# Six transformer layers behind a cross attention: the layer loop written out, a new order of work in each slot, one half of the LayerNorm read in place

## What is computed

```python
x = x + tanh(g_xattn[0]) * xattn(layernorm(x), ctx, ctx, frac, ...)      # logits + alpha_pos*max(D,0) + alpha_neg*min(D,0), D = clip(frac_k - frac_q)
y = layernorm(x)
for i in range(6):
    y = attn_layer(shift_tokens(y), Wqkv[i], q_scale[i], k_scale[i], Wo[i]) + y
    y = ffn_layer(shift_tokens(y), ln_g[i], ln_b[i], W1[i], b1[i], W2[i], b2[i]) + y
x = x + tanh(g_ffn[0]) * y
# shift_tokens: the first 64 features of a token stay, the last 64 come from the token before
# attn_layer: 16 heads of 64; q and k are divided by their norms, scaled and rotated; each window of
#             32 tokens looks at itself and at the window before it; softmax; Wo
# ffn_layer: LayerNorm, W1 (2 x 341 columns), a * gelu(gate), W2
```

## Time and profile before

| | |
|---|---|
| median of three runs | 2069.49 us (2068.37 to 2073.53) |
| profiled execution, its own time | 2061.48 us |
| span from its first to its last instruction | 2059.7 us |
| PE busy / weight loads | 1797.2 us (87%) / 1401.8 us (68%) |
| VectorE / ScalarE / GpSimd busy | 1600.0 (78%) / 1384.6 (67%) / 1332.1 (65%) us |
| cross attention, about | 0 to 250 us |
| a layer, about | 297 to 299 us, six times |

### The profile page before, as it was taken

How to read it: one execution, slowest core, us unless ns; L and a number is a source line. 1 busy time by engine, 2 the same in 40 slices (tenths; PEclk the granted TensorE clock), 3 DMA queues, 4 the chain that set the end, 5 groups by cost and what they waited for, 6 DMA issues and landing times.

```text
span 2059.7 us, 86637 instructions
## 1 busy us (share of the span) xinstructions
PE 1797.2 (87%) x33584; PEld 1401.8 (68%) x33584; DVE 1600.0 (78%) x3772; ACT 1384.6 (67%) x3701; POOL 1332.1 (65%) x1226
## 2 busy tenths in 40 slices
PE   6999878998879898789988899988898988899887
PEld 3445457777667776677776677776677776677766
DVE  5766679898468987488896589885689885689984
ACT  3677657777557776567775577775577775577765
POOL 3444467777467777377775477774677773677773
PEclk9999979999989999999999999999899999899999
DMA  5000021111021111111110211110211110211111
GB/s 121 4 5 5 1 70 33 35 37 32 25 64 41 31 36 28 63 34 33 40 31 23 68 40 31 41 31 23 64 44 31 31 42 22 65 37 37 31 33 46
DMA packets 59120, 77.81 MB, mean 38 GB/s; under 512 B 16608, under 2 KB 31674, under 8 KB 57914
## 3 DMA queue, kind: packets, MB, share of 16 engines
q1 hardware_dynamic: 58938, 75.36, 13.9%
HBM read 22.63 MB, written 1.05 MB: 11 GB/s over the span
## 4 chain that ended last, share of the span: by engine, by line
PE 60%; DVE 15%; issue 12%; ACT 6%; POOL 5%; SPq 0%; DMA 0%; DVEq 0%; ACTq 0%; POOLq 0%
PE proj_ps L455 7%; PE s_ps L476 7%; PE tr_ps L465 7%; PE y_ps L524 7%; PE proj_ps L457 5%; PE proj_ps L456 5%; PE y_ps L516 4%; DVE by_cos L1091 3%; PE pv_ps L506 3%; ACT square L816 3%; DVE by_sin L1091 3%; DVE xs L1352 3%; PE s_ps L571 3%; DVE sumsq L1103 2%; PE s_ps L691 2%
## 5 line engine op out<-in xcount | busy, mean ns | idle before, releaser
L1502 POOL TENSOR_TENSOR qk<-by_cos,by_sin 128x512 f32<-128x512 f32 x388 | 495.3, 1276 | 208.3 <-DVE by_sin L1091 201.9
L1509 POOL TENSOR_TENSOR qk<-qk,inv_norm 128x512 f32<-128x512 f32 x388 | 404.8, 1045 | 68.7 <-ACT inv_norm L822 41.6
L1091 DVE TENSOR_TENSOR by_cos<-proj_ps,tab 128x512 f32<-128x512 f32 x364 | 249.4, 685 | 159.6 <-ACT square L816 158.6
L816 ACT ACTIVATE square<-proj_ps 128x512 f32<-128x512 f32 x364 | 217.4, 597 | 195.1 <-PE proj_ps L457 194.8
L1515 POOL TENSOR_TENSOR s_sb<-s_sb,row_max 128x512 f32<-128x512 f32 x192 | 202.7, 1056 | 136.1 <-DVE row_max L1122 136.1
L455 PE MATMUL proj_ps<-w_hi,x_hi 128*128 128x512 f32 x546 | 273.8, 502 | 4.8 <-DVE by_sin L1091 2.6
L465 PE MATMUL tr_ps<-ident,qk 128*128 128x128 f32 x1544 | 247.2, 284 | 24.2 <-ACT x_hi L810 11.8
L1103 DVE TENSOR_REDUCE sumsq<-square 128x8 f32<-128x512 f32 x388 | 262.2, 676 | 0.0
L1091 DVE TENSOR_TENSOR by_sin<-proj_ps,tab 128x512 f32<-128x512 f32 x364 | 247.8, 681 | 0.0
L465 PEld LDWEIGHTS tr_ps<-ident,qk 128*128 128x128 f32 x1544 | 184.0, 146 | 72.5 <-POOL qk L1509 28.5
L457 PE MATMUL proj_ps<-w_hi,x_lo 128*128 128x512 f32 x546 | 222.1, 407 | 0.0
(11 more groups left out here) (172 smaller groups left out, 4167.1 us busy)
## 6 DMA issues: line engine op xcount, KB each, us to landing
arena<-v SPq DMA_DIRECT2D x388, 130.0 KB, 2.4
w_raw<-in_L_ffn_Wqkv SPq DMA_DIRECT2D x7, 1536.0 KB, 7.3
wo<-in_L_ffn_Wo SPq DMA_DIRECT2D x7, 512.0 KB, 3.8
w_raw<-in_L_ffn_W SPq DMA_DIRECT2D x7, 341.0 KB, 5.5
c_in<-in_ctx SPq DMA_DIRECT2D x16, 64.0 KB, 1.8
xn<-in_fside_BxS SPq DMA_DIRECT2D x1, 1024.0 KB, 6.0
out<-z SPq DMA_DIRECT2D x4, 256.0 KB, 3.0
w<-in_L_ffn_W SPq DMA_DIRECT2D x12, 64.0 KB
```

Source lines behind the costliest of these rows:

```text
L1091: return dve.tensor_tensor(dst[:, c % 2, :].rearrange("p (h d) -> p h d", d=DH), ps, tb, ALU.mult)
L1502: pool.tensor_tensor(heads(qk[:, c, :]), heads(by_cos[:, c % 2, :]), heads(by_sin[:, c % 2, :])[:, :, ::-1, :], ALU.add).then_inc(qk_added, 1)
L1509: pool.tensor_tensor(ap, ap, inv_norm[:, c, :].unsqueeze(2).to_broadcast([128, 8, DH]), ALU.mult).then_inc(qk_ready, 1)
```

## The change

1. `for L in range(1, LAYERS + 1)` in place of `Fori` on all five engines: six copies of a layer's code in a row. The loops over the six pairs of slots inside a layer stay loops.
2. The order of the calls in a layer's slot is another on PE, ScalarE, VectorE and GpSimd. On VectorE `step` is dissolved.
3. The LayerNorm reads the unshifted half from `z` itself: the copy at L1352 goes, the statistics are taken in two instructions of 64 columns and joined by `bn_aggr`, and `ln_apply` is two `scalar_tensor_tensor` of 64 columns, with the inverse deviation as a broadcast tensor input. `xs_ready` is raised once a sequence.
4. Cross attention: `x_scores` is called for 0 and for 2 only and makes two groups: bias g, logits g, logits g + 1, bias g + 1. The wait for the copy-out of group g - 1 now stands ahead of the logits of group g.

```diff
-        stats = sb("stats", [128, 2, 6])
+        stats = sb("stats", [128, 2, 2, 6])
@@ every engine
-            with pe.Fori(1, LAYERS + 1) as L:
+            for L in range(1, LAYERS + 1):
@@ cross attention, PE
+            def x_bias(T, par, g, first):
+                hi, lo = flat(pos_hi[:, GH * g:GH * g + GH]), pos_lo[g]
+                pe.matmul(s_ps[:, g % 2, :], d_hi[:, par], hi, start=first, stop=False)
+                pe.matmul(s_ps[:, g % 2, :], d_hi[:, par], lo, start=False, stop=False)
+                return pe.matmul(s_ps[:, g % 2, :], d_lo[:, par], hi, start=False, stop=not first)
+            def x_logits(T, par, g, first):
+                rows = slice(32 * g, 32 * g + 32)
+                return pe.matmul(s_ps[:, g % 2, :], xq[rows, par, :], flat(xk_bd[rows, par]), start=first, stop=not first)
...
+                if after(T, 1) or g >= 2:
+                    pe.wait_ge(masked, T * 4 + g)
+                x_logits(T, par, g, False).then_inc(s_full, 1)
+                x_logits(T, par, g + 1, True)
+                x_bias(T, par, g + 1, False).then_inc(s_full, 1)
@@ x_slot, PE
-                x_scores(T, par, 1)
...
-                x_scores(T, par, 3)
@@ VectorE
                 def ln_stats(T, n, par):
-                    zt = tile_of(z, n, 0, D // 2)
                     dve.wait_ge(sh_full, T + 1)
-                    dve.tensor_scalar(xs[:, par, 0:D // 2], zt, 1.0, None, ALU.mult).then_inc(xs_ready, 1)
-                    dve.tensor_copy(xs[:, par, D // 2:D], y_ps[:, 0:D // 2]).then_inc(xs_ready, 1)
-                    dve.wait_ge(xs_ready, T * 2 + 2)
-                    dve.bn_stats(stats[:, par], xs[:, par]).then_inc(stat_done, 1)
+                    dve.tensor_copy(xs[:, par], y_ps[:, 0:D // 2]).then_inc(xs_ready, 1)
+                    dve.bn_stats(stats[:, par, 0], tile_of(z, n, 0, D // 2))
+                    dve.wait_ge(xs_ready, T + 1)
+                    dve.bn_stats(stats[:, par, 1], xs[:, par]).then_inc(stat_done, 1)
                 def ln_apply(T, n, par):
-                    dve.tensor_scalar(tile_of(xn, n), xs[:, par],
-                                      mean_var[:, par, 0:1], rstd[:, par:par + 1], ALU.subtract, ALU.mult).then_inc(xn_ready, 1)
+                    for lo, src in ((0, tile_of(z, n, 0, D // 2)), (D // 2, xs[:, par])):
+                        last = dve.scalar_tensor_tensor(tile_of(xn, n, lo, lo + D // 2), src, mean_var[:, par, 0:1],
+                                                        rstd[:, par:par + 1].to_broadcast([128, D // 2]), ALU.subtract, ALU.mult)
+                    last.then_inc(xn_ready, 1)
```

More of the change, by code:

```diff
@@ L599, in x_slot @@
                     x_values(T - 1, 1 - par, 1)
-                x_scores(T, par, 1)
-                if not first:
                     x_p_transpose(T - 1, 3)
@@ L705, in slot @@
                         p_transpose(T - 1, 1)
-                    if behind >= 2:
-                        shift_state(T - 2, tile_of(z, n - 2, D // 2))
+                    if front_on:
+                        project(T + 1, 1)
                     if first:
@@ L710, in slot @@
                     qk_transpose(T, 3)
-                    if front_on:
-                        project(T + 1, 1)
+                    if behind >= 2:
+                        shift_state(T - 2, tile_of(z, n - 2, D // 2))
                     if behind >= 1:
                         values(T - 1, 1 - par, 1)
-                        att_transpose(T - 1, 0)
                     if front_on:
                         project(T + 1, 2)
-                        qk_transpose(T + 1, 0)
+                    if behind >= 1:
+                        att_transpose(T - 1, 0)
                     scores(T, par, 1)
+                    if not front_on:
+                        f_transpose(0, tr_ps)
                     if front_on:
                         project(T + 1, 3)
-                    else:
-                        f_transpose(0, tr_ps)
-                    p_transpose(T, 0)
+                        qk_transpose(T + 1, 0)
                     if behind >= 1:
                         att_transpose(T - 1, 1)
+                    p_transpose(T, 0)
                     if front_on:
@@ L731, in slot @@
                         qk_transpose(T + 1, 1)
+                        project(T + 1, 5)
                     values(T, par, 0)
-                    if front_on:
-                        project(T + 1, 5)
-                        if not last_front:
-                            x_transpose(T + 2)
+                    if front_on and not last_front:
+                        x_transpose(T + 2)
                     if behind >= 1:
@@ L954, in _ @@
                 qk_out(NB, 0, c)
-            with act.Fori(1, LAYERS + 1) as L:
+            for L in range(1, LAYERS + 1):
                 def f_out(j, ps=pt_ps):
@@ L1341, in _ @@
             dve.wait_ge(param_ld, N_PARAM)
-            with dve.Fori(1, LAYERS + 1) as L:
+            for L in range(1, LAYERS + 1):
                 def add_out(T, n):
@@ L1401, in slot @@
                         w_round(0, L + 1)
[L1402 removed]
+                    if front_on:
+                        times_cos(T + 1, 0, L - 1)
+                        sum_squares(T + 1, 0)
+                        times_sin(T + 1, 0, L - 1)
+                        clamp_norm(T + 1, 0)
+                    if behind >= 2:
+                        ln_stats(T - 2, n - 2, par)
+                    if front_on:
+                        times_cos(T + 1, 1, L - 1)
+                        times_sin(T + 1, 1, L - 1)
+                        sum_squares(T + 1, 1)
@@ L1403, in slot @@
+                    if behind >= 1:
+                        sums_inverse(T - 1, 1)
+                    if behind >= 2:
+                        dve.wait_ge(stat_done, T - 1)
+                    if behind >= 1:
+                        normalise(T - 1, 1)
                     if behind >= 2:
                         ln_variance(T - 2, par)
+                    if front_on:
+                        clamp_norm(T + 1, 1)
+                    mask(T, 1)
+                    if not front_on:
+                        w_round(1, L + 1)
@@ L1584, in _ @@
             scale_rotated(NB, 3)
-            with pool.Fori(1, LAYERS + 1) as L:
+            for L in range(1, LAYERS + 1):
                 def slot(T, n, par, first=False, behind=2, front_on=True, last_front=False):
@@ L1590, in slot @@
                         pool.tensor_tensor(w1_lo[:], w1_raw[:], w1_hi[:].bitcast(f32), ALU.subtract).then_inc(w1_split, 1)
-                    for g in range(NG):
-                        if g == 0:
-                            if not first:
-                                scale_rotated(T, 3)
-                        elif front_on:
-                            scale_rotated(T + 1, g - 1)
-                        if g % 2 == 0:
-                            center(T, g // 2)
-                        if not front_on and 1 <= g < 3:
-                            w_rest(g - 1, L * 3 + g)
-                        if front_on:
-                            if g == 3 and not last_front:
-                                split_x(T + 2)
-                            add_rotated(T + 1, g)
+                    if not first:
+                        scale_rotated(T, 3)
+                    center(T, 0)
+                    if not front_on:
+                        w_rest(0, L * 3 + 1)
+                    if front_on:
+                        add_rotated(T + 1, 0)
+                        scale_rotated(T + 1, 0)
+                        add_rotated(T + 1, 1)
+                        scale_rotated(T + 1, 1)
+                        add_rotated(T + 1, 2)
+                    center(T, 1)
+                    if not front_on:
+                        w_rest(1, L * 3 + 2)
+                    if front_on:
+                        scale_rotated(T + 1, 2)
+                    if front_on and not last_front:
+                        split_x(T + 2)
+                    if front_on:
+                        add_rotated(T + 1, 3)
                 layer_slots(pool.Fori, L, slot)
```

99 lines of the change are left out of this document (43 added, 56 removed).

## The result

| | |
|---|---|
| after, median of four runs | 1914.95 us (1913.99 to 1919.0) |
| before, median of four runs beside them | 2068.93 us (2061.25 to 2073.53) |
| ratio, with its 95% interval | 0.9263 (0.9232 to 0.9294) |
| profiled execution after, its own time / span | 1919.0 / 1916.2 us |

1950 us were predicted, 1910 to 2010; the change gives 154 us, and 119 were forecast. The time lies 5 us above the low end of the range.

A forecast was written before the change was run, and what follows sets the result against it. PE and VectorE, both near their limit, were held by waits, with layer starts a bound of their own. Savings of 78 + 24 + 10 + 7 = 119 off 2061.5, plus 8, gave 1950 us, range 1910 to 2010.

The forecast's parts named there:

- Full slots: Layers' 78 full slots: with PE's wait for xs gone, 14.4 us each, 78 us saved (ends 0 and 103).
- the wait for `xs`: Full slots: PE's 1.32 us wait goes, as project 2 delays PE 0.8 us and VectorE loses a 0.7 us copy.
- Start of the layers: Start of layers 2 to 6: ten issue gaps go (24 us) and the slow clock behind them (10 us).
- that of the half clock: Start of layers 2 to 6: PE need not run at half clock behind the gaps; 2 us a layer, 10 us.
- Slots 0, 1, 14, 15 and tails: First and last slots and tails of the layers: same work, taken as 0, ends 6 us either way.
- Cross attention: 16 cross-attention slots: two logits products side by side, most given back; 14 x 0.5, 7 us (-7 to +13).
- Rival A: Full slots: VectorE waits for GpSimd in ln_apply; if both halves wait, slots gain nothing, 2028 us; chance 0.10.
- its first branch: Rival A with one wait of at most 1.28 us in ln_apply: VectorE 14.5 us, nearly nothing lost.
- Its second branch: Rival A with both halves of ln_apply waiting, up to 2.2 us: VectorE 15.4 us, slots gain nothing, 2028 us.
- B: Slots: another wait takes half the gain, 39 us less from the slots, 1989 us; chance 0.17.
- C: Layer starts: the written-out loop does not take the gaps away, 34 us less gain, 1984 us; chance 0.08.
- D: Inner loops: their branch back stalls about 4 us in 36 passes, costing 146 us, 2096 us; chance 0.07.

The follow-up runs named there:

- e4: Kernel before with only the new order of work on PE, ScalarE, VectorE and GpSimd in the layers' slots: 1965.4 us, ratio 0.9520.
- e8: Changed kernel without the LayerNorm in place (copy into xs, one statistics instruction, one ln_apply put back): 1918.4 us, ratio 0.9291.
- e2: Kernel before with only the LayerNorm in place, old order of work: 2082.43 us, ratio 1.0102.
- e1: Kernel before with only the loop over the six layers written out: 2024.93 us, ratio 0.9798.
- e3: Kernel before with only the pairs of logits in the cross attention: 2052.75 us, ratio 0.9940.
- e9: Changed kernel with the sine product ahead of the sum of squares for chunk 0 on VectorE: 1942.72 us, ratio 0.9397.
- e12: Changed kernel with x_att_out earlier in cross attention, sine before sum for chunk 0, ln_apply behind chunk 3's cosine and sum: 1881.72 us, ratio 0.9124.
- e7: Changed kernel with each half of ln_apply as a tensor_scalar with one tensor input: 1917.6 us, ratio 0.9290.
- the second edit: Changed kernel with x_att_out ahead of the exponentials of group 2 on ScalarE in the cross attention: 1892.52 us, ratio 0.9147.
- e6: Changed kernel with both halves of ln_apply issued a second time, into a tile nobody reads: 1994.59 us, ratio 0.9668.

## Why the prediction was right, point by point

- **Full slots.** Forecast 14.4 us and 78 us in sum; measured 14.38, and 72.0 between the traces (the forecast took 1.0 for each of 78 slots, though its own 15.36 - 14.4 is 0.96; it is 0.92 over the 13 intervals of a layer). VectorE's work came out at 13.9 us, not 13.2, for the wait in `ln_apply`. The next wait was named rightly (`qk_transpose(T+1, 1)`), the second one (sine of chunk 0) was missed.
- **Why the wait for `xs` goes.** Here the step was wrong: "VectorE's way to `xs` loses the copy of 0.7 us". e4 and e8 keep that copy in the code and have the same slots; e2 takes it away in the old order and gains 0.14 us in most slots and loses 0.7 in others. The order does it, and it does it twice over: it brings `project 2` ahead of the waiting transpose, and it moves the copy into a pause of GpSimd, where it takes 183 ns.
- **Start of the layers.** Forecast 34 us; e1 gave 42, the traces 48 in the changed kernel. Some of this is the order's, which the forecast did not count there: e4 keeps the loop and shortens the same five stretches by 10 us. The term of the gaps (24) could be read off; that of the half clock (10, ends 0 and 20) was too small: e1 leaves 42 - 24 = 18 for it and for what else ran late behind the gaps, which these runs don't separate.
- **Slots 0, 1, 14, 15 and tails.** Forecast 0 within 6; measured 1.9 in layer 1's start and 16.3 for slot 15 and the tails, 18 in all, the largest error of the sum and outside its ends. These gain with the new order too (e4's layer is 16.4 us shorter, of which 12.0 lie in the 13 intervals); which waits did it was not followed.
- **Cross attention.** Forecast 7 us, 4.5 in the trace of after; e3's runs gave 12 (8 to 17), its trace 7.3, so the term is known only roughly. Side by side was right. Not seen: PE's idle time there takes the granted clock down to about 0.9.
- **Rival A.** The wait in `ln_apply` is there, once a slot, 998 ns, and hidden, as its first branch said. The sign named for A, a mean above 600 ns, came up all the same (650 ns over all instructions of both halves) while A's price did not: one long wait is enough for it, so the sign could not tell the two branches apart. Nor is one wait sure: in most slots of e2 neither half waits. Its second branch (both halves wait) came true in e9, at 14.84 us a slot. The argument against that branch, "between two halves GpSimd must be ready with a new operation each time", was weak: its pause is 0.24 us.
- **B, C, D.** B: the new waits are 0.5 us a slot together, within the forecast's slot. C and D fell with e1. (A pair of slots has 1418 PE instructions by the earlier trace rows, not some 1300; nothing hangs on it.)
- **How close it was.** The mechanism was forecast in the main, the size less well. The terms missed by -6 us (full slots), +14 (starts), +18 (slots 0, 1, 15 and tails) and -2.5 (cross attention), 24 in sum, and the 8 us added for the median should have been 12 us less. The low end of the range was built on 103 us from the full slots, which gave 72; that the time is inside it, by 5 us, is in part luck.

## What to carry to other kernels

Where VectorE and GpSimd share a slot, look for VectorE's small operations that live in SBUF alone (copies, staging, normalisation) and read what GpSimd does at their start. The same half of `ln_apply` took 0.28 or 1.15 us in e2 for a few nanoseconds of timing. Moving such operations to another place (e4, and e12 with its swap) gained; taking one out or changing its form (e2, e7, e8) gained nothing. An order of work on several engines is one object: change it on all of them at once, and after any swap look at the whole list of waits and at the medians of the small operations again. When a change frees an engine (the pairs of logits), look at once for the ring that now holds the slot; there the second edit gave more than the first.

## What was not expected of the hardware

- A return to the head of a long outer loop cost 8.4 us in all for each of the five returns, though the issue pieces sum to 5.1: the rest stands behind them, half of the clock included. Six copies of the code in a row made no gap over 1 us in the layers.
- A one-input `tensor_scalar` from SBUF to SBUF waits for GpSimd as a two-input operation does (968 and 998 ns for 64 columns, 999 for the single one of 128 in e4).
- The outcome of that race hangs on a few nanoseconds: in e2 every second half that began 28 ns or more ahead of GpSimd went through, and those of 22 to 24 ns ahead were held for 0.87 us. In e6 the border lay at about 20 ns.
- In the cross attention the granted clock of the 50 us shown fell from 1.00 (2.4 GHz throughout) to a mean of 0.93 (some of it at 1.2 GHz) once the pairs of logits left PE idle between its pieces, and was back at 1.00 when `x_att_out` came earlier.
